# Moving the transposes of the next x, and their evictions, between the second and the third V product

## The chip, the cores and the metric

The kernel runs on one core of a Trainium2 chip. The metric is the device time of one execution in microseconds (us), the median of the runs shown.

## The reference

One layer of gated cross-attention and a quantised feed-forward, for 8 batches of 512 rows and 512 columns (8 x 512 x 512), 16 heads of 32:

```
x = x + tanh(g_xattn) * xattn(layernorm(x), ctx, ctx)
x = x + tanh(g_ffn)   * ffn(layernorm(x))

xattn(query, key, value):
    Q, K, V = query Wq' + bq, key Wk' + bk, value Wv' + bv      # per head
    scores = Q K' / sqrt(32)
    feats  = mean(scores), mean of row maxima, variance of softmax(scores)
    t      = exp(clip(mlp(feats)))                              # one per head
    out    = softmax(Q K' / (2 t)) V
    return out Wo' + bo
ffn(x): quant_act(gelu(quant_act(x) ternary(w1)')) ternary(w2)'
```

## The kernel before

**Turns.** The work on a batch is split into three parts, and a turn `i` does three of them at once: the scores and their statistics for batch `i` (`has_a`), the second scores, values, output product and feed-forward for batch `i - 1` (`has_b`), and the normalisation and the K, V and Q products for batch `i + 1` (`has_p`). Turn -1 has only the products (start-up), turn 0 has no `has_b`, turns 1 to 6 are a hardware loop and have all parts (the text calls them looped turns one to six), turns 7 and 8 have no products. Each engine has its program written out by hand in `body`; nothing is reordered later, and engines meet at semaphores.

**Score tiles.** A score tile is one matmul of 128 x 512 into one of two banks `a_ps` (`score_a`, L1157), its negated row maximum on VectorE (`row_max`, L822), its exponential on ScalarE (`first_exp`, L655) and its statistics on VectorE (`row_stat`, L827). TensorE waits before tile k for the exponential of tile k - 2. Forty of the 64 tiles of a batch run beside the second scores; the rest are "dense": `tiles_a(point)` places 1 or 2 of them ahead of or inside each of the 16 products of a turn, on all three engines in the same order.

**The products.** Behind the second scores come four K products, four output products W0 to W3 (with `has_b`), then the transposes of x and the V products, and four Q products. A K, W, V or Q product is 12 matmuls of 128 x 512 (`split_product`, L1138: high and low halves of fp16 pairs). Between the second and third Q product come the transposes of the quantised residual, `xq`. Each of these writes one of four PSUM banks in turn (`mm_ps` 0 and 1, `b_ps` 0 and 1, in this order banks 0 to 3). `bank_uses` lists the uses of a turn in order and `mm_use` gives for each the bank and how often it was used before: TensorE waits in `take` on `mm_free` of the bank, and the engine that empties it waits on `mm_full`. This list is what sets the bank of a product; the order of the code must agree with it.

**x.** VectorE normalises the next x tile by tile (`norm_x`, L914 and L916), GpSimd makes the low half (`split_x`, L588, `x_lo_done`) and between them adds the output product to the residual (L610). TensorE turns the four tiles (X0 to X3, L1250), 8 transposes of 128 x 128 for each, high and low halves, into one bank, and ScalarE evicts each into `xT` with one instruction of 128 x 1024 (L721). The Q products read `xT` and start when all four are drained. The V products read only the context (`c_hi`, `c_lo`); ScalarE evicts them into `vbuf` (L730).

**VectorE beside the V products.** After the last `norm_x` it takes the statistics of the residual (L883, L1068), then the row maximum of V0's score tile, then the normalised residual (`norm_residual`, L892), the row maximum of V1's tile, the quantisation (`quantise_x`, L897 to L903), and the row maxima of V2's and V3's tiles.

TensorE's order before, in words, per turn: K0 to K3, W0 to W3, X0 to X3, V0 to V3, Q0, Q1, xq, Q2, Q3. ScalarE's: the evictions in the same order, each V eviction behind the exponential of its product's score tile:

```
for t in range(T) if has_p else ():          # X0..X3, L718
    act_waits.wait_ge(mm_full[bank_n], before + 1)
    nc.scalar.activation(xT[...], mm_16[bank_n], ACT.Copy).then_inc(mm_free[bank_n], 1)
for t in range(T):                           # V0..V3, L725
    tiles_a(C + T + t)
    ...
    nc.scalar.activation(vbuf[1 - par][:, t, :], mm_ps[bank_n][:, :], ACT.Copy, ...)
```

Of the kernel before, what the change touches and what calls it, by code (L numbers as in the profile page):

```python
# [31 lines left out]
T = S // P  # L32
# [74 lines left out]
def bank_uses(setup, has_p, has_b, has_a):  # L107

    def some(stage, count, present=True):
        return [(stage, k) for k in range(count)] if present else []  # L110

    uses = some("S", 1, setup == 0) + some("K", C, has_p) + some("W", T, has_b)
    uses += some("X", T, has_p) + some("V", T, has_p)
    uses += some("Q", C, has_p)[:2] + some("xq", T, has_b) + some("Q", C, has_p)[2:]
    uses += some("S", 1, setup == -1)
    uses += some("up0", NB, has_b) + some("up1", NB, has_b) + some("M", 2, has_a)
    for t in range(T):
        if has_b:
            uses += some(f"turn{t}", 2)
            if t > 0:  # L120
                uses += [(f"down{t - 1}", 0)]
            if t + 2 < T:
                uses += some(f"up{t + 2}", NB)
        if has_a and t < 2:
            uses += [("M", 2 + t)]
    uses += some(f"down{T - 1}", 1, has_b)
    return {use: n for n, use in enumerate(uses)}


USES = {-1: bank_uses(-1, True, False, False), 0: bank_uses(0, True, False, True),  # L130
        1: bank_uses(None, True, True, True), 7: bank_uses(None, False, True, True),
        8: bank_uses(None, False, True, False)}
# [11 lines left out]
def mm_use(i, stage, k=0):  # L144

    if isinstance(i, int) and not 1 <= i <= 6:
        n = STARTS[i] + USES[i][stage, k]
        return n % MM, n // MM
    n = STARTS[1] + USES[1][stage, k]
    return n % MM, (i - 1) * (USES_ALL // MM) + n // MM  # L150


def nth(b, per, k):


    return (b + 1) * per + k
# [30 lines left out]
def stages(i):  # L187

    if isinstance(i, int):
        return 0 <= i < B, 1 <= i <= B, i + 1 < B  # L190
    return True, True, True


def flamingo_kernel(nc, x, ctxT, g_xattn, g_ffn, WqT, bq, WkT, bk, WvT, bv, WoT, bo,
                    w1T, b1, w2T, b2, w3T, b3, f1T, f2T, out):
    with ExitStack() as ctx:
# [184 lines left out]
        def dense_tiles(i, point):  # L381

            sets, dense = a_plan(i)
            first = sets + sum(dense[:point])
            return range(first, first + dense[point])
# [243 lines left out]
        def _(act):  # L629
# [21 lines left out]
            def first_exp(b, k):  # L651
                n, t = k // T, k % T
                act_waits.wait_ge(a_max, nth(b, H * T, k + 1))
                act_waits.wait_ge(a_stat, nth(b, H * T, k - 1))
                nc.scalar.activation(etile[:, k % 2, :], a_ps[k % 2][:, :], ACT.Exp,  # L655
                                     bias=nmax[:, slot_of(n), t:t + 1], scale=1.0).then_inc(a_exp, 1)
# [11 lines left out]
            def body(i, par):  # L668
                has_a, has_b, has_p = stages(i)
# [12 lines left out]
                def tiles_a(point):  # L682
                    for k in dense_tiles(i, point) if has_a else ():
                        first_exp(i, k)
# [26 lines left out]
                for t in range(T):  # L711
                    tiles_a(C + t)
                    if has_b:
# [1 line left out]
                        act_waits.wait_ge(mm_full[bank_n], before + 1)  # L715
                        nc.scalar.activation(attn[:, t, :], mm_ps[bank_n][:, :], ACT.Copy,
                                             scale=tg_w[:, 0:1]).then_inc(mm_free[bank_n], 1)
                for t in range(T) if has_p else ():  # L718
                    bank_n, before = mm_use(i, "X", t)
                    act_waits.wait_ge(mm_full[bank_n], before + 1)  # L720
                    nc.scalar.activation(xT[:, :, :, t * P:(t + 1) * P].rearrange("p l c n -> p (l c) n"),  # L721
                                         mm_16[bank_n], ACT.Copy).then_inc(mm_free[bank_n], 1)
                if isinstance(i, int) and i == 0:
                    act_waits.wait_ge(f_tern, 7)
                for t in range(T):  # L725
                    tiles_a(C + T + t)
                    if has_p:
                        bank_n, before = mm_use(i, "V", t)
                        act_waits.wait_ge(mm_full[bank_n], before + 1)
                        nc.scalar.activation(vbuf[1 - par][:, t, :], mm_ps[bank_n][:, :], ACT.Copy,  # L730
                                             scale=1.0 / WSCALE).then_inc(mm_free[bank_n], 1)
# [381 lines left out]
        def _(pe):  # L1113
# [3 lines left out]
            def take(i, stage, k=0):  # L1117

                bank_n, before = mm_use(i, stage, k)
                if not (isinstance(before, int) and before == 0):  # L1120
                    pe_waits.wait_ge(mm_free[bank_n], before)
                return bank_n
# [5 lines left out]
            def split_product(bank_n, left, right, tiles=()):  # L1128


                tiles = list(tiles)
                if tiles:
                    tiles.pop(0)()
                pairs = [(c, l, r) for c in range(C) for l, r in ((0, 0), (0, 1), (1, 0))]
                for c, l, r in pairs:
                    if tiles and (c, l, r) == pairs[len(pairs) // 2]:
                        tiles.pop(0)()
                    ins = mat(mm_ps[bank_n][:, :], left[l](c), right[r](c),  # L1138
                              start=(c, l, r) == pairs[0], stop=(c, l, r) == pairs[-1])
                ins.then_inc(mm_full[bank_n], 1)  # L1140
# [48 lines left out]
            def body(i, par):  # L1189
                has_a, has_b, has_p = stages(i)  # L1190
# [24 lines left out]
                def tiles_a(point):  # L1215
                    return [lambda k=k: score_a(i, par, k) for k in dense_tiles(i, point)] if has_a else []

                def alone(tiles):
                    for tile in tiles:
                        tile()  # L1220
# [16 lines left out]
                for t in range(T):  # L1237
# [3 lines left out]
                                      [lambda c, w=w: w["o"][:, c, :] for w in (w_hi, w_lo)], tiles_a(C + t))  # L1241
                    else:
                        alone(tiles_a(C + t))
                if has_p:
                    for t in range(T):
                        pe_waits.wait_ge(x_lo_done, nth(i + 1, T, t + 1))
                        bank_n = take(i, "X", t)
                        for l in range(2):
                            for c in range(C):
                                ins = nc.tensor.transpose(mm_16[bank_n][:, l * C + c, :],  # L1250
                                                          x_split[t][:, l, c * P:(c + 1) * P], ident16[:, :])
                        ins.then_inc(mm_full[bank_n], 1)
                if first:
                    pe_waits.wait_ge(w_lo_done, 2)
                for t in range(T):
                    rows = slice(t * P, (t + 1) * P)
                    if has_p:
                        split_product(take(i, "V", t), [lambda c, x=x: x(c, rows) for x in c_parts],
                                      [lambda c, w=w: w["v"][:, c, :] for w in (w_hi, w_lo)], tiles_a(C + T + t))
                    else:  # L1260
                        alone(tiles_a(C + T + t))
# [127 lines left out]
```

## Time and profile before

| what | value |
|---|---|
| median of 3 runs | 1525.43 us (1525.19 to 1525.73) |
| span of the profiled execution, first to last instruction | 1523.1 us (its time outside the span is not given apart; the median is 2.3 us above the span) |
| TensorE busy | 1247.1 us (82%), 6620 matmuls |
| VectorE busy | 1187.1 us (78%) |
| ScalarE busy | 958.2 us (63%) |
| GpSimd busy | 429.1 us (28%) |
| mean granted TensorE clock | 0.911 of full speed |

PE is TensorE (PEld its weight loads), DVE VectorE, ACT ScalarE, POOL GpSimd, SP SyncE, whose queue issues the DMAs. Times within the trace count from the first instruction. L1138 is line 1138 of the kernel. `region` stands for several buffers: at L1250 the source `region` is the first half of the x pairs and `x_more` the second half, at L721 `region` is `xT`. Matmuls are pipelined: a row of one matmul shows 0.38 us at full clock while the next starts 0.217 us after it.

### The profile page before, as it was taken

Reading aid. Unit: us, or ns where it says so; the run is one execution under the profiler, and the core shown is the slowest. Engines: PE = TensorE matmul, PEld = TensorE weight load, DVE = VectorE, ACT = ScalarE, POOL = GpSimd, SP = SyncE. Lnnn points to the kernel's source line nnn. Section 1 sums busy time; section 2 is a strip of 40 time slices with the busy share of each in tenths; the row PEclk is TensorE's granted clock in tenths of the full one; section 3 lists DMA queues with packets and bytes.
Section 4 is the critical chain, followed back from the end, with each engine's and each line's share of the span. In section 5 each row is a group of like instructions: output and inputs, shape, how many; then the busy total and the mean of one; then the engine's idle time right before and its main releaser. Section 6 shows DMA issues by size and latency. Waiting matters only on the chain.

```text
span 1523.1 us, 23233 instructions
## 1 busy us (share of the span) xinstructions
PE 1247.1 (82%) x6620; PEld 450.7 (30%) x6620; DVE 1187.1 (78%) x2082; ACT 958.2 (63%) x1559; POOL 429.1 (28%) x389
## 2 busy tenths in 40 slices
PE   3635669988898889988898889988998899778958
PEld 1201321244213332244214331244213431133224
DVE  7399769888788958888788959888688969974236
ACT  3554469755785559755785659755795658744814
POOL 5350342331325212331325213331225211210220
PEclk9855779999999999999999999999999999879979
DMA  8250130012202110012202110112202110001000
GB/s 320 63 159 0 42 86 12 30 41 50 76 2 70 43 72 15 34 37 56 70 2 70 43 72 15 37 34 52 74 2 70 43 56 1 1 0 57 1 0 28
DMA packets 34977, 73.66 MB, mean 48 GB/s; under 512 B 7456, under 2 KB 7456, under 8 KB 34336
## 3 DMA queue, kind: packets, MB, share of 16 engines
q1 hardware_dynamic: 34848, 72.10, 16.1%
q8 instruction: 62, 1.02, 0.3%
q14 instruction: 67, 0.55, 0.1%
HBM read 38.39 MB, written 8.39 MB: 31 GB/s over the span
## 4 chain that ended last, share of the span: by engine, by line
PE 44%; DVE 32%; issue 12%; ACT 6%; POOL 4%; DVEq 1%; DMA 1%; SPq 0%; ACTq 0%; POOLq 0%
DVE stat L827 7%; PE mm_ps L1138 6%; PE b_ps L1312 5%; DVE nmax L822 5%; PE b_ps L1163 5%; PE a_ps L1157 4%; PE b_ps L1138 4%; PE mm_ps L1178 4%; PE mm_ps L1185 3%; ACT etile L655 3%; PE o_ps L1178 3%; PE mm_ps L1291 2%; DVE hmax L952 2%; POOL xres L610 2%; PE b_ps L1291 2%
## 5 line engine op out<-in xcount | busy, mean ns | idle before, releaser
L655 ACT ACTIVATE etile<-a_ps,nmax 128x512 f32<-128x512 f32 x512 | 355.8, 697 | 251.7 <-DVE nmax L822 250.7
L822 DVE TENSOR_REDUCE nmax<-a_ps 128x1 f32<-128x512 f32 x512 | 348.8, 682 | 89.1 <-PE a_ps L1157 81.4
L665 ACT ACTIVATE region<-b_ps,inv2t 128x512 f32<-128x512 f32 x512 | 333.6, 700 | 66.9 <-PE b_ps L1163 63.3
L827 DVE BATCH_NORM_STATS2 stat<-etile 128x6 f32<-128x512 f32 x512 | 350.7, 685 | 15.5 <-ACT etile L655 13.2
L1157 PE MATMUL a_ps<-kst,qst 96*128 96x512 f16 x512 | 213.3, 418 | 105.8 <-ACT etile L655 80.7
L1163 PE MATMUL b_ps<-qst,kst 97*128 97x512 f16 x512 | 198.7, 398 | 24.1 <-ACT region L665 15.1
L583 POOL TENSOR_TENSOR region<-region 128x512 f16<-128x512 f32 x64 | 80.7, 1263 | 307.4 <-ACT region L702 307.2
L1163 PEld LDWEIGHTS b_ps<-qst,kst 97*128 97x128 f16 x512 | 49.3, 97 | 287.5 <-ACT region L665 254.4
L544 POOL TENSOR_TENSOR region<-region 128x512 f32<-128x512 f32 x32 | 40.5, 1267 | 325.2 <-DVE region L855 325.2
L569 POOL TENSOR_TENSOR xres<-xres,bo_row 128x512 f32<-128x512 f32 x32 | 39.7, 1273 | 318.0 <-DMA xres<-in_x_dram 318.0
L1157 PEld LDWEIGHTS a_ps<-kst,qst 96*128 96x128 f16 x512 | 50.6, 99 | 211.1 <-ACT etile L655 168.0
L1312 PE MATMUL b_ps<-f,region 128*128 128x512 fp8e4 x496 | 110.8, 379 | 0.0
L952 DVE TENSOR_REDUCE hmax<-region 128x1 f32<-128x512 f32 x128 | 80.6, 678 | 9.2 <-ACT region L762 8.2
L1178 PE MATMUL mm_ps<-region,vbuf 128*32 128x512 f32 x512 | 73.8, 650 | 0.0
L762 ACT ACTIVATE region<-mm_ps,xmax 128x512 f32<-128x512 f32 x64 | 42.8, 691 | 49.1 <-PE mm_ps L1291 48.8
L1291 PE MATMUL mm_ps<-f,region 128*128 128x512 fp8e4 x256 | 70.0, 421 | 4.3 <-ACT region L745 1.8
L1178 PE MATMUL o_ps<-region,vbuf 128*32 128x512 f32 x512 | 68.2, 605 | 2.3 <-ACT region L665 2.1
L1185 PE MATMUL mm_ps<-region,ones 128*32 128x512 f32 x512 | 70.0, 620 | 0.0
L1185 PE MATMUL z_ps<-region,ones 128*32 128x512 f32 x512 | 68.0, 603 | 0.0
L1291 PE MATMUL b_ps<-f,region 128*128 128x512 fp8e4 x256 | 61.8, 382 | 1.8 <-DVE region L975 1.6
L1312 PEld LDWEIGHTS b_ps<-f,region 128*128 128x128 f16 x496 | 47.5, 98 | 53.1
L981 DVE SCALAR_TENSOR_TENSOR xres<-b_ps,out_scale,xres 128x512 f32<-128x512 f32 x31 | 23.2, 749 | 46.5 <-PE b_ps L1312 46.4
(218 smaller groups left out, 2038.1 us busy)
## 6 DMA issues: line engine op xcount, KB each, us to landing
kst<-region SPq DMA_DIRECT2D x96, 128.0 KB, 2.3
qst<-region SPq DMA_DIRECT2D x96, 128.0 KB, 2.3
region<-in_x_dram SPq DMA_DIRECT2D x8, 1024.0 KB, 5.4
xres<-in_x_dram SPq DMA_DIRECT2D x8, 1024.0 KB, 5.2
out_dram<-xres SPq DMA_DIRECT2D x32, 256.0 KB, 2.0
cin<-in_ctxT_dram SPq DMA_DIRECT2D x30, 256.0 KB, 5.1
kst<-in_f1T_dram SPq DMA_DIRECT2D x2, 1024.0 KB, 11.2
qst<-in_f2T_dram SPq DMA_DIRECT2D x2, 1024.0 KB, 5.4
```

The source lines that it names most:

```text
L655: nc.scalar.activation(etile[:, k % 2, :], a_ps[k % 2][:, :], ACT.Exp, bias=nmax[:, slot_of(n), t:t + 1], scale=1.0).then_inc(a_exp, 1)
L665: nc.scalar.activation(probs[:, s % 2, g, :], b_ps[g % 2][:, :], ACT.Exp, scale=inv2t[:, slot:slot + 1]).then_inc(b_exp, 1)
L822: vec.tensor_reduce(nmax[:, slot_of(k // T), k % T:k % T + 1], a_ps[k % 2][:, :], AX.X, ALU.max, negate=True).then_inc(a_max, 1)
L827: vec.bn_stats(stat[:, slot_of(k // T) * T + k % T, :], etile[:, k % 2, :]).then_inc(a_stat, 1)
L952: ins = vec.tensor_reduce(hmax[:, n:n + 1], hbuf[t % 2][:, n * S:(n + 1) * S], AX.X, ALU.max, apply_absolute_value=True)
L1138: ins = mat(mm_ps[bank_n][:, :], left[l](c), right[r](c), start=(c, l, r) == pairs[0], stop=(c, l, r) == pairs[-1])
L1157: mat(a_ps[k % 2][:, :], qst[par][0:SHIFT, slot, t * P:(t + 1) * P], kst[par][0:SHIFT, slot, :], start=True, stop=True).then_inc(a_full, 1)
L1163: mat(b_ps[g % 2][:, :], kst[par][0:SHIFT + 1, slot, k * P:(k + 1) * P], qst[par][0:SHIFT + 1, slot, :], start=True, stop=True).then_inc(b ...
L1178: mat(oz_ps[G % 2][0][g * DK:(g + 1) * DK, :], vbuf[par][:, k, n * DK:(n + 1) * DK], probs[:, s % 2, g, :], start=k == 0, stop=k == T - 1)
L1185: ins = mat(oz_ps[G % 2][1][g * DK:(g + 1) * DK, :], ones32[:, 0:DK], probs[:, s % 2, g, :], start=k == 0, stop=k == T - 1)
L1291: ins = mat(mm_ps[bank_n][:, :], xqT[:, c, t * P:(t + 1) * P], f1[:, c, n * S:(n + 1) * S], start=c == 0, stop=c == C - 1)
L1312: ins = mat(mm_ps[bank_n][:, :], hT[t % 2][:, k, :], f2[:, k, :], start=k == 0, stop=k == KC - 1)
```

## The change

The four uses "X" move in the bank list from in front of the first V to between the second and the third V. On TensorE the loop over the transposes becomes a function that is called ahead of the third V product (and of its score tile), and on ScalarE the loop over the x evictions becomes a function that is called ahead of the exponential of the third V product's score tile. Nothing else is edited; behind these places the line numbers grow by 4 on ScalarE and TensorE, and by 7 on TensorE behind the loop (L1138 is now L1142, L1250 is L1254, L730 is L734).

```diff
@@ bank_uses
     uses = some("S", 1, setup == 0) + some("K", C, has_p) + some("W", T, has_b)
-    uses += some("X", T, has_p) + some("V", T, has_p)
+    uses += some("V", T, has_p)[:2] + some("X", T, has_p) + some("V", T, has_p)[2:]
     uses += some("Q", C, has_p)[:2] + some("xq", T, has_b) + some("Q", C, has_p)[2:]
@@ scalar
-                for t in range(T) if has_p else ():
+                def turned_x(t):
                     bank_n, before = mm_use(i, "X", t)
                     act_waits.wait_ge(mm_full[bank_n], before + 1)
                     nc.scalar.activation(xT[:, :, :, t * P:(t + 1) * P].rearrange("p l c n -> p (l c) n"),
                                          mm_16[bank_n], ACT.Copy).then_inc(mm_free[bank_n], 1)
+
                 if isinstance(i, int) and i == 0:
                     act_waits.wait_ge(f_tern, 7)
                 for t in range(T):
+                    if has_p and t == 2:
+                        for n in range(T):
+                            turned_x(n)
                     tiles_a(C + T + t)
@@ tensor
-                if has_p:
+                def turned_x():
                     for t in range(T):
                         pe_waits.wait_ge(x_lo_done, nth(i + 1, T, t + 1))
                         bank_n = take(i, "X", t)
...
                         ins.then_inc(mm_full[bank_n], 1)
+
                 if first:
                     pe_waits.wait_ge(w_lo_done, 2)
                 for t in range(T):
                     rows = slice(t * P, (t + 1) * P)
+                    if has_p and t == 2:
+                        turned_x()
                     if has_p:
                         split_product(take(i, "V", t), ...
```

ScalarE in a looped turn, from the last output product's eviction (L716) to the x evictions; `mm_ps0` and `mm_ps1` are banks 0 and 1, `b_ps0` and `b_ps1` banks 2 and 3. This is the difference, where + is the change:

```order
 L716 ACTIVATE region1<-b_ps1,tg_w 128x512 [waits mm_full3]
 L97 REGISTER_ALU
+L97 REGISTER_ALU [waits a_max]
+L655 ACTIVATE etile<-a_ps0,nmax 128x512 [waits a_stat]
+L97 REGISTER_ALU
+L734 ACTIVATE vbuf1<-mm_ps0 128x512 [waits mm_full0]
+L97 REGISTER_ALU
+L97 REGISTER_ALU [waits a_max]
+L655 ACTIVATE etile<-a_ps1,nmax 128x512 [waits a_stat]
+L97 REGISTER_ALU
+L734 ACTIVATE vbuf1<-mm_ps1 128x512 [waits mm_full1]
+L97 REGISTER_ALU
```

Two exponentials and the evictions of V0 and V1 now stand between W3's eviction and X0's.

TensorE in a looped turn, behind W3's last matmul, before the change (L1250 are the transposes, the first two groups of four):

```order
L1138 MATMUL b_ps1<-wo_hi,region4 128x512
L97 REGISTER_ALU
L97 REGISTER_ALU [waits x_lo_done]
L1250 MATMUL mm_ps0<-ident16,region3 128x128 [waits mm_free0]
L1250 MATMUL mm_ps0<-ident16,region3 128x128 x7
L97 REGISTER_ALU
L97 REGISTER_ALU [waits x_lo_done]
L1250 MATMUL mm_ps1<-ident16,region3 128x128 [waits mm_free1]
```

and behind V1's last matmul, with the change (the last two groups of four, and V2's score tile and first product):

```order
L1254 MATMUL mm_ps0<-ident16,x_more 128x128 [waits mm_free0]
L1254 MATMUL mm_ps0<-ident16,x_more 128x128 x7
L97 REGISTER_ALU
L97 REGISTER_ALU [waits x_lo_done]
L1254 MATMUL mm_ps1<-ident16,x_more 128x128 [waits mm_free1]
L1254 MATMUL mm_ps1<-ident16,x_more 128x128 x7
L97 REGISTER_ALU
L97 REGISTER_ALU [waits mm_free2]
L1161 MATMUL a_ps0<-kst0,qst0 128x512 [waits a_exp]
L1142 MATMUL b_ps0<-wv_hi,c_hi 128x512
```

The transposes stood behind W3 and took banks 0 to 3 in this order; now V0 and V1 take banks 0 and 1, X0 and X1 banks 2 and 3, X2 and X3 banks 0 and 1, and V2 and its tile wait for bank 2, which X0 filled.

## Rows read from the trace of the kernel before

**Rows 1.** The page's chain that ended last, share of the span by engine.
```profile
PE 44%; DVE 32%; issue 12%; ACT 6%; POOL 4%; DVEq 1%; DMA 1%; SPq 0%; ACTq 0%; POOLq 0%
```

**Rows 2.** The chain in order of time, looped turn four: start, us, what.
```profile
830.71 0.70 DVE st L883
...
841.57 0.61 DVE nmax L822
...
844.93 1.30 PE mm_ps L1138 x6
```

**Rows 3.** Timeline of TensorE, turn four: start, us, engine, line, op, tiles, count [idle before].
```profile
824.13 1.06 PE L1250 MATMUL mm_ps<-ident,region 128*128 128x128 f16 x16
826.38 0.62 PE L1250 MATMUL b_ps<-ident,x_more 128*128 128x128 f16 x8 [1.20 <-POOL x_more L588]
829.58 1.03 PE L1250 MATMUL b_ps<-ident,x_more 128*128 128x128 f16 x8 [2.58 <-POOL x_more L588]
...
830.83 0.63 PE L1138 MATMUL mm_ps<-wv_hi,c_hi 128*128 128x512 f16 x1
831.26 0.63 PE L1138 MATMUL mm_ps<-wv_lo,c_hi 128*128 128x512 f16 x1
...
843.03 0.39 PE L1157 MATMUL a_ps<-kst,qst 96*128 96x512 f16 x1
843.25 0.60 PE L1138 MATMUL mm_ps<-region,wq_hi 128*128 128x512 f16 x2
```

**Rows 4.** Timeline of ScalarE, turn four, W3's score tile to V2's.
```profile
826.33 0.69 ACT L655 ACTIVATE etile<-a_ps,nmax 128x512 f32<-128x512 f32 x1 [1.93 <-DVE nmax L822]
...
827.49 1.94 ACT L721 ACTIVATE region<-mm_ps 128x1024 f16<-128x1024 f16 x2
...
832.61 0.69 ACT L655 ACTIVATE etile<-a_ps,nmax 128x512 f32<-128x512 f32 x1 [0.94 <-DVE nmax L822]
...
836.44 0.69 ACT L655 ACTIVATE etile<-a_ps,nmax 128x512 f32<-128x512 f32 x1 [1.26 <-DVE nmax L822]
837.39 0.60 ACT L730 ACTIVATE vbuf<-mm_ps 128x512 f32<-128x512 f32 x1 [0.27 <-PE mm_ps L1138]
842.28 0.69 ACT L655 ACTIVATE etile<-a_ps,nmax 128x512 f32<-128x512 f32 x1 [4.29 <-DVE nmax L822]
```

**Rows 5.** Timeline of VectorE, turn four.
```profile
833.60 1.92 DVE L892 TENSOR_SCALAR region<-xres,mv,rstd 128x512 f32<-128x512 f32 x4 [0.50 <-POOL rstd L556]
835.63 0.69 DVE L822 TENSOR_REDUCE nmax<-a_ps 128x1 f32<-128x512 f32 x1
```

**Rows 6.** Timelines of VectorE and TensorE, turns two and five.
```profile
490.70 1.92 DVE L892 TENSOR_SCALAR region<-xres,mv,rstd 128x512 f32<-128x512 f32 x4 [0.50 <-POOL rstd L556]
500.36 0.60 PE L1138 MATMUL mm_ps<-region,wq_hi 128*128 128x512 f16 x2
...
1002.61 0.63 PE L1138 MATMUL mm_ps<-wv_hi,c_hi 128*128 128x512 f16 x1
1005.38 1.92 DVE L892 TENSOR_SCALAR region<-xres,mv,rstd 128x512 f32<-128x512 f32 x4 [0.49 <-POOL rstd L556]
1015.95 0.59 PE L1138 MATMUL mm_ps<-region,wq_hi 128*128 128x512 f16 x2
```

**Rows 7.** Timelines of ScalarE and TensorE, the turn of batch 0.
```profile
171.67 0.69 ACT L655 ACTIVATE etile<-a_ps,nmax 128x512 f32<-128x512 f32 x1 [1.42 <-DVE nmax L822]
...
176.53 1.03 PE L1250 MATMUL b_ps<-ident,x_more 128*128 128x128 f16 x8 [1.07 <-POOL x_more L588]
...
190.53 0.60 PE L1138 MATMUL mm_ps<-region,wq_hi 128*128 128x512 f16 x2
```

**Rows 8.** Timelines of TensorE and ScalarE, start-up: first transposes, key eviction, last V eviction.
```profile
31.67 1.06 PE L1250 MATMUL b_ps<-ident,region 128*128 128x128 f16 x16
37.26 0.86 PE L1250 MATMUL mm_ps<-ident,x_more 128*128 128x128 f16 x8 [4.54 <-ACT region L702]
...
39.43 0.58 PE L1138 MATMUL b_ps<-wv_hi,c_hi 128*128 128x512 f16 x1
...
37.67 0.69 ACT L702 ACTIVATE region<-mm_ps,bqk 128x512 f16<-128x512 f32 x1
...
50.68 0.60 ACT L730 ACTIVATE vbuf<-mm_ps 128x512 f32<-128x512 f32 x1 [1.99 <-PE mm_ps L1138]
```

## The prediction

> **What bounds the kernel now.** First the page's chain: the last-ending work is 44% TensorE and 32% VectorE [rows 1], so the two engines share the bound and a gap on TensorE costs only where no VectorE chain ends behind it. Then the chain in order of time through one looped turn, the fourth of six [rows 2]: from the residual's statistics at 830.71 it runs through VectorE and GpSimd up to the row maximum at 841.57, then changes to TensorE, and stays on TensorE's query products, six matmuls in 1.30 us (0.217 us each, at 2.4 GHz). So the query stage starts when both are ready, and from there its start moves everything behind it.
>
> Then the timelines of that stretch, one engine at a time. TensorE [rows 3]: the x transposes begin at 824.13, and two of the four groups wait for GpSimd's low halves (1.20 and 2.58 us). The V products begin at 830.83 at the lower clock (0.43 us from one to the next), and the query stage's score tile comes at 843.03. ScalarE [rows 4]: the x evictions run from 827.49, the exponentials of the V stage's first, second and third tile at 832.61, 836.44 and 842.28. VectorE [rows 5]: the residual's normalisation starts at 833.60, the second V tile's row maximum at 835.63. The turn's VectorE order holds the score tiles back, and ScalarE evicts V0 only behind the first of these exponentials and V1 only behind the second.
>
> **The change, part by part.** Nothing is added or removed: 32 transposes and 4 evictions change places per batch, and so do the banks. No DMA moves, and SP's queue, GpSimd and VectorE keep their order; their waits for bank releases get other numbers. V0 and V1 keep the first two of the four banks, X0 and X1 take the third and fourth, X2 and X3 the first and second again (which V0 and V1 must have left), V2 and V3 the third and fourth (which X0 and X1 must have left).
>
> *The six looped turns.* What is taken away: TensorE no longer stands 1.20 and 2.58 us for GpSimd in front of V0. V0 starts at 824.2. Its 13 steps (a tile and 12 products) last 2.8 us, V1's tile is let go by the exponential that ends at 827.02 [rows 4], and V1 ends near 829.9. X0 and X1 are ready by then and end near 831. What is added: X2 needs V0's eviction, which comes behind the exponential at 832.61, and X3 needs V1's, behind the one at 836.44. Neither can come earlier, since VectorE's order in front of them is unchanged. TensorE therefore stands some 3 us twice. And the x evictions now queue behind V1's: from the row maximum at 835.63 it is 0.81 us to the exponential, 0.59 to V1's eviction (as from 836.44, one instruction to the next), 0.60 for it [rows 4], 1.03 for X0's (an x eviction by itself, as the two at 827.49 last 1.94 with 0.9 between their starts), and 0.06 to TensorE, as between the exponential's end at 842.97 and the tile at 843.03. So V2, whose bank X0 held, starts 3.1 us behind that row maximum, at 838.7. X3's transposes (8 in 0.52 to 0.86 us from 837.7) are done by then.
>
> Behind that stand V2, V3 and the query tile: 27 steps of 0.217 us, 5.85 us, plus what the clock takes. Before, the 52 steps from the first V product to the first query product, 11.3 us at full clock, took 13.34 us in turn five (1002.61 to 1015.95) [rows 6] and 12.42 in turn four (830.83 to 843.25, the latter 0.22 behind the tile); so restarts cost 1.2 to 2.1 us there, after 2.58 us of standing. Now TensorE has done only 32 transposes in the 8.8 us ahead of V2. I take 1.6 us, with 0 and 5.7 (all 27 steps at 0.43) as far bounds. The first query product then comes 2.03 + 3.1 + 5.85 + 1.6 = 12.58 us behind the start of the residual's normalisation (2.03 is 833.60 to 835.63). For turn four: 846.18 in place of 843.25, 2.93 later. Turns one, three and six repeat turn four within 0.1 us. Turn two: 490.70 + 12.58 = 503.28 against 500.36, 2.92 later. Turn five: 1005.38 + 12.58 = 1017.96 against 1015.95, 2.01 later [rows 6]. Sum over six turns: **+16.6 us**. Nothing hides it: queued on TensorE behind the two waits are V2, V3 and the whole query stage, and for that wait ScalarE's evictions, GpSimd's low halves and the feed-forward. On ScalarE the exponential of V2's tile is queued behind the four x evictions; they end near 841.3, before its row maximum is due (841.57), so it stays where it was.
>
> *The turn of batch 0*, which has no output product and no residual. TensorE stood between the transpose groups for GpSimd, the last from 176.53, and reached the query products at 190.53 [rows 7]. Now V0's tile can start when the exponential of 171.67 has ended, at 172.4; 26 steps, at the lower clock for the first 4.2 us (a loss of 2.1, as in turn five), end near 180.2. V0 and V1 are evicted as they end, for VectorE has no residual work there. The 32 transposes take 2.1 us, V2 starts at 182.4, the first query product comes 5.85 us later, at 188.3: **-2.2 us** (bounds -1 and -3).
>
> *The start-up.* TensorE ended the key products and the first transposes at 32.7 and stood until 37.26, when ScalarE had emptied a key bank; V began at 39.43 and its last eviction at 50.68, behind which ScalarE's start-up chain runs without a gap [rows 8]. Now V0 and V1 fill 31.7 to 36.9. The last key eviction ends at 38.36; V0's, V1's and X0's end at 40.4; V2 starts at 40.5 and V3 ends 5.2 us later, 45.7, plus 0 to 1.7 us at the lower clock. V3's eviction starts near 46.5: **-4.2 us** (bounds -3.2 and -4.8). The chain behind it is ScalarE's sums and VectorE's ternary weights, whose data have landed, so the gain is kept.
>
> Sum: -4.2 - 2.2 + 16.6 = +10.2 us. The trace's span is 1523.1 us, 2.3 under the median of the runs, 1525.4; I keep that difference. **1535.6 us.**
>
> The clock is the one price where a page speaks. In the trace it was at 1.2 GHz after GpSimd's waits, and back at 2.4 by the query products [rows 2, 3]. The Trainium skill, TensorE: Matmul & The Clock Gate, section "A second HAM failure mode: psum-queue depth-cycling", says that short idle times between groups of matmuls which cycle through PSUM banks make the clock swing, and that the work between them pays for it; by that rule the clock's share would grow with this change, which speaks against it. The first rival gives the same mechanism its price from rows.
>
> **The rivals.** (a) *The clock stays down through V2 and V3.* TensorE now has two long waits in a row where it had shorter ones, and enters V2 after 8.8 us with little work. All 27 steps at 0.43 us in place of 0.217 add 5.7 us, not 1.6: 4.1 more in each of six turns, 24.6, and 1560.2 us. Against it: in no turn before did a restart cost more than 2.1 us. Chance 0.08.
>
> (b) *No bank wait: the new place only fills the gap.* If V0 and V1 were out of their banks when TensorE reaches X2 (at 831), TensorE would be at the query tile by 841 and wait for the exponential of 842.28, as now. The looped turns would gain 0 in four, 0.2 in turn two, 0.9 in turn five, and with the two early stages the sum is -7.5: 1517.9 us, faster. It decides at one point: V1's exponential would have to end before 831 instead of at 837.1, so VectorE would have to take its row maximum ahead of the residual's statistics. The order says that it doesn't. What speaks for it is that two waits of 1.20 and 2.58 us do vanish. Chance 0.08.
>
> (c) *The losses are small and the two early stages pay for them.* If V2 and V3 ran at full clock (no 1.6), each turn loses 1.3 (turn five 0.4), 7.0 in all, and the sum is +0.6: 1526.0 us. For it: V0 and V1 now run at full clock. Against it: after less standing than now, the clock was down in every turn. Chance 0.14 (all that ends within 0.2%).
>
> The change does what it says in any case: both engines' orders show it in all eight batches' turns.
>
> **How the numbers follow.** My forecast has 0.70, (a) 0.08, (b) 0.08, (c) 0.14. 0.2%, 3.05 us, is about what a measurement of this kernel can tell from no change. The forecast's own range takes 0.9 to 2.6 us for the clock (6 times -0.7 and +1.0) and the bounds of the early stages: 1530 to 1544. To hold 8 in 10 it must reach half-way to (c) and a little into (a): 1528 to 1547. Faster by over 0.2%: 0.08; within: 0.14; slower: 0.78.
>
> **What would show it.** In a looped turn: V0 starting right behind W3; X2 and X3 waiting for ScalarE's V evictions, some 3 us each; V2's first product 5 us behind the residual's normalisation; four x evictions in a row behind V1's; the query tile waiting for TensorE itself and no longer for the exponential; each looped turn about 2.8 us longer. Batch 0's turn and the start-up shorter by 2 and 4 us. I am wrong if V2 starts before ScalarE has done X0, if the exponentials of the first two V tiles come earlier, or if the query stage starts where it did.

## The result and the profile after

| | before | after |
|---|---|---|
| median of 5 runs each, taken on the same chip | 1525.73 us (1525.19 to 1529.63) | 1536.91 us (1535.29 to 1539.35) |
| ratio of after to before, 95% interval (from all the runs; the two medians by themselves give 1.0073) | | 1.0066 (1.0048 to 1.0084) |
| span of the profiled execution (own time of after's: 1539.35 us) | 1523.1 us | 1537.6 us |
| TensorE busy, VectorE busy | 1247.1, 1187.1 us | 1250.8, 1189.7 us |
| first query product behind the start of the residual's normalisation, mean of six looped turns | 9.81 us | 12.69 us |
| first query product of the start-up | 50.48 us | 46.73 us |
| first output product of turn one | 300.74 us | 296.04 us |

The change makes the kernel slower, by 11.2 us between the medians. The profiled execution of after is the slowest of its five, so its trace shows somewhat more: 14.5 us of span. Runs of the kernel before spread from 1524.5 to 1531.1 us over the chips used here; its trace [rows 1 to 8], with a span of 1523.1 us, is one of the faster ones, while its medians in the comparisons below lie between 1525.4 and 1528.1. So small effects are read from the stages of the traces, and from ratios only with their intervals.

The chain that ended last, by engine, is almost that of before [rows 1]; a share over the whole span doesn't tell what moved. The profile page of after:

```profile
PE 43%; DVE 32%; issue 12%; ACT 6%; POOL 4%; DVEq 1%; DMA 1%; SPq 0%; ACTq 0%; POOLq 0%
```

The list of TensorE's waits tells it (what waited, for whom: us in total, times, longest). Of after:

```profile
PE a_ps L1161 <- ACT etile L655: 84.9, 88, 8.4
PE mm_ps L1254 <- ACT vbuf L734: 35.8, 12, 3.2
```

The first line, of score tiles, was about as long before (80.7 us); the second is new. And in the same list of before stood the wait that the change was to take away:

```profile
PE b_ps L1250 <- POOL x_more L588: 25.3, 14, 2.6
```

The 25.3 us of waiting for GpSimd are gone, and 35.8 us of waiting for ScalarE's evictions of V0 and V1 have come: twelve of them, two in each looped turn.

Looped turn four on TensorE after the change (start, us, engine, line, op, tiles, count, idle before it and who ended it), against [rows 3]:

```profile
830.65 0.38 PE L1142 MATMUL mm_ps<-wv_hi,c_hi 128*128 128x512 f16 x1
...
836.20 1.06 PE L1254 MATMUL b_ps<-ident,region 128*128 128x128 f16 x16
840.16 0.62 PE L1254 MATMUL mm_ps<-ident,x_more 128*128 128x128 f16 x8 [2.91 <-ACT vbuf L734]
843.98 1.03 PE L1254 MATMUL mm_ps<-ident,x_more 128*128 128x128 f16 x8 [3.20 <-ACT vbuf L734]
844.97 0.61 PE L1161 MATMUL a_ps<-kst,qst 96*128 96x512 f16 x1
845.37 0.63 PE L1142 MATMUL b_ps<-wv_hi,c_hi 128*128 128x512 f16 x1
...
848.23 0.38 PE L1142 MATMUL b_ps<-wv_lo,c_hi 128*128 128x512 f16 x1
...
852.12 0.38 PE L1161 MATMUL a_ps<-kst,qst 96*128 96x512 f16 x1
852.34 0.59 PE L1142 MATMUL mm_ps<-region,wq_hi 128*128 128x512 f16 x2
```

V0 starts behind W3 without a wait, V1 and the transposes of X0 and X1 follow without one; then TensorE stands twice, for X2's bank and for X3's. V2's tile comes at 844.97, at the lower clock, and the query tile at 852.12 has nothing in brackets: it waits for TensorE alone.

ScalarE in the same stretch, against [rows 4]:

```profile
838.93 0.69 ACT L655 ACTIVATE etile<-a_ps,nmax 128x512 f32<-128x512 f32 x1 [5.03 <-DVE nmax L826]
839.52 0.59 ACT L734 ACTIVATE vbuf<-mm_ps 128x512 f32<-128x512 f32 x1
842.75 0.69 ACT L655 ACTIVATE etile<-a_ps,nmax 128x512 f32<-128x512 f32 x1 [2.65 <-DVE nmax L826]
843.34 0.59 ACT L734 ACTIVATE vbuf<-mm_ps 128x512 f32<-128x512 f32 x1
843.81 1.94 ACT L721 ACTIVATE region<-b_ps 128x1024 f16<-128x1024 f16 x2
845.62 1.96 ACT L721 ACTIVATE region<-mm_ps 128x1024 f16<-128x1024 f16 x2
848.60 0.69 ACT L655 ACTIVATE etile<-a_ps,nmax 128x512 f32<-128x512 f32 x1 [1.01 <-DVE nmax L826]
```

V0 and V1 were finished on TensorE at 833.4 and 836.4, and ScalarE empties them at 839.52 and 843.34. It had stood idle for 5.03 and 2.65 us ahead of the exponentials in front of them. The two exponentials wait for VectorE, against [rows 5]:

```profile
839.91 1.91 DVE L896 TENSOR_SCALAR region<-xres,mv,rstd 128x512 f32<-128x512 f32 x4 [0.50 <-POOL rstd L556]
841.95 0.69 DVE L826 TENSOR_REDUCE nmax<-a_ps 128x1 f32<-128x512 f32 x1
...
847.80 0.68 DVE L826 TENSOR_REDUCE nmax<-a_ps 128x1 f32<-128x512 f32 x1
849.72 0.69 DVE L826 TENSOR_REDUCE nmax<-a_ps 128x1 f32<-128x512 f32 x1 [0.64 <-PE a_ps L1161]
```

VectorE itself is as far in its order as before: 2.04 us from the residual's normalisation to V1's row maximum, as in [rows 5]. The last row is V3's tile, for which it now waits 0.64 us.

The chain in order of time (start, us, what) strings the three together, against [rows 2]:

```profile
841.95 0.70 DVE nmax L826
...
843.34 0.60 ACT vbuf L734
...
843.98 1.03 PE mm_ps L1254 x8
845.02 0.56 PE a_ps L1161
845.58 3.89 PE b_ps L1142 x12
849.47 0.22 PE a_ps L1161
849.69 2.59 PE b_ps L1142 x12
852.28 0.22 PE a_ps L1161
852.50 1.30 PE mm_ps L1142 x6
```

Before, the chain changed from VectorE to TensorE at V2's row maximum, with the query products next [rows 2]. Now it leaves VectorE one tile earlier, at V1's, goes through ScalarE's eviction of V1, and has X3, V2 and V3 between that and the query products. V2's twelve products last 3.89 us and V3's 2.59: of the first, 1.30 us is clock.

### The profile page after: what moved, and what is told of

Read it like the earlier page. It is cut to its first block, busy times and chain, and to the rows that moved or that the text cites. A ratio compares the mean times of both kernels' runs of the same rounds, so it can differ in the third digit from the quotient of the medians.

```text
span 1537.6 us, 23233 instructions
## 1 busy us (share of the span) xinstructions
PE 1250.8 (81%) x6620; PEld 450.9 (29%) x6620; DVE 1189.7 (77%) x2082; ACT 957.2 (62%) x1559; POOL 428.1 (28%) x389
## 4 chain that ended last, share of the span: by engine, by line
PE 43%; DVE 32%; issue 12%; ACT 6%; POOL 4%; DVEq 1%; DMA 1%; SPq 0%; ACTq 0%; POOLq 0%
DVE stat L831 7%; DVE nmax L826 5%; PE b_ps L1319 5%; PE b_ps L1167 5%; PE b_ps L1142 5%; PE mm_ps L1142 5%; PE a_ps L1161 4%; PE mm_ps L1182 4%; PE mm_ps L1189 3%; ACT etile L655 3%; PE o_ps L1182 2%; PE mm_ps L1298 2%; POOL xres L610 2%; DVE hmax L956 2%; PE b_ps L1298 2%
## 5 line engine op out<-in xcount | busy, mean ns | idle before, releaser
L1167 PE MATMUL b_ps<-qst,kst 97*128 97x512 f16 x512 | 198.0, 396 | 24.2 <-ACT region L665 15.2
L985 DVE SCALAR_TENSOR_TENSOR xres<-b_ps,out_scale,xres 128x512 f32<-128x512 f32 x31 | 23.2, 749 | 46.5 <-PE b_ps L1319 46.4
```

The costliest lines, as they stand in the source:

```text
L1167: mat(b_ps[g % 2][:, :], kst[par][0:SHIFT + 1, slot, k * P:(k + 1) * P], qst[par][0:SHIFT + 1, slot, :], start=True, stop=True).then_inc(b ...
```

## The experiments

Each result below is a median, beside the median of the kernel before on the same chip. Line numbers differ by a few from kernel to kernel. The time from the start of the residual's normalisation to the first query product, in a looped turn, is called the **query delay**: 9.65 us before (10.57 in turn five), 12.2 to 13.1 after.

### The change in the two early stages alone, and in the looped turns alone

`has_b` is true in the looped turns and false in the start-up and batch 0's turn. In the first kernel the transposes move only there:

```diff
-                    if has_p and t == 2:
+                    if has_p and t == (2 if not has_b else 0):
                         turned_x()
```

(with the same condition in ScalarE's loop and in `bank_uses`), and in the second the condition is turned round.

> Only the turns without a value part (start-up and batch 0) have the transposes of x and their evictions behind the second V product; the six looped turns are as before the change. Theory (two gains, one loss): the start-up and batch 0's turn end 4.7 us earlier, as in the trace of the change, and the looped turns take what they took: about 1520.7 us, 4.7 under the kernel before. Rival (the gain of the early turns is taken up by a later wait, or the trace's 4.7 us is clock chance): within 1.5 us of the kernel before.

Measured: 1522.58 us beside 1528.14, ratio 0.9968 (0.9955 to 0.9981), 5.6 us faster, near the 4.7 expected. In its trace the first output product of turn one comes at 292.60, 8.1 us earlier than before, but the span is only 2.3 us shorter (1520.8 us): the query delay is 9.66 us in three looped turns and 10.6 to 10.8 in the other three, 2.2 us more in sum, and the stages behind it take 3.6 us more. In those three turns it is 13.4 to 13.6 us from the first V product to the first query product, as in turn five before (13.34 [rows 6]); why is open.

> Only the six looped turns have the change; start-up and batch 0's turn are as before it. Theory: each looped turn loses 2.5 to 3.5 us between the residual's normalisation and the first query product, 17.3 in all, so 15 to 18 us over the kernel before, about 1542 us, and 4 to 5 us over the change. Rival (the loss depends on what the early turns do, by the phase of the clock): no more than 11 us over the kernel before, as the whole change.

Measured: 1542.45 us beside 1528.14, ratio 1.0093 (1.0077 to 1.0108), 14.3 us slower, a little less than the 15 to 18 expected. The query delays sum to 75.77 us, against 76.12 after the whole change and 58.84 before.

So the change is two changes of opposite sign, and the sum of the two, +8.7 us between the medians, is near the 11.2 of the whole (by the ratios, +0.61% against +0.66%). The gain of the early stages varies from trace to trace: in the eight traces here that have the new place there, the first output product of turn one lies between 292.60 and 296.04.

### Is it the wait for the two banks, or ScalarE's order?

The profile names the waits of X2 and X3. Here these two get banks of their own, in `o_ps` and `z_ps`, which are idle beside these products, and TensorE no longer waits for banks 0 and 1 there; ScalarE reads the new banks in the same order, and nothing else moves:

```diff
-                        bank_n = take(i, "X", t)
+                        bank_n = take(i, "X", t) if t < 2 else mm_use(i, "X", t)[0]
+                        turned = mm_16[bank_n] if t < 2 else oz_16[t - 2]
```

> The change, with the transposes of the third and fourth x tile written to two PSUM banks that are idle there (those of the last heads' outputs and denominators), so that TensorE doesn't wait for the evictions of V0 and V1; ScalarE's order is that of the change. Theory T2 (ScalarE's order is the price: X0's eviction, and so V2's bank, comes behind the exponential of V1's score tile): V2 still starts 3 us behind the second tile's row maximum, the time stays within 2 us of the change, about 1537 us; the two waits of 2.9 and 3.2 us become one wait in front of V2. Theory T1 (TensorE's waits for the banks of V0 and V1 are the price): V2 starts right behind the transposes, the looped turns lose nothing, and the time is 1518 to 1522 us.

Measured: 1537.15 us beside 1528.14, ratio 1.0055 (1.0041 to 1.0069). TensorE in turn four of this kernel:

```profile
833.67 1.06 PE L1257 MATMUL b_ps<-ident,region 128*128 128x128 f16 x16
834.56 0.61 PE L1257 MATMUL o_ps<-ident,x_more 128*128 128x128 f16 x8
835.01 0.61 PE L1257 MATMUL z_ps<-ident,x_more 128*128 128x128 f16 x8
842.45 0.60 PE L1163 MATMUL a_ps<-kst,qst 96*128 96x512 f16 x1 [6.83 <-ACT region L722]
```

Both waits are gone and one of 6.83 us stands in their place, in front of V2, for X0's eviction. The query delays sum to 77.76 us, no less than with the change. The two waits that were new in the list were not what the time hung on. (Turn six alone lost more than with the change, 13.81 us of delay against 12.15, at a mean granted clock of 0.65 from V2's tile to the query products, against 0.81.)

The next kernel adds to this one ScalarE's order: in the looped turns it evicts X0 to X3 behind V0 and ahead of V1's exponential. (GpSimd adds the bias to V0 and V1 when their banks are released; since the x evictions now stand ahead of V1's and count on the same semaphores, GpSimd waits for one release more. This is in the edit too.)

```diff
-                    if has_p and t == 2:
+                    if has_p and t == (1 if has_b else 2):
```

> As the run with two more banks, and in the looped turns ScalarE evicts the four x tiles behind V0's eviction and ahead of the exponential of V1's score tile. Theory T2: V2's bank is free some 1.2 us behind the start of the residual's normalisation in place of 5, V2 and V3 end before the exponential of V2's score tile, and the query tile waits for it, 9.4 us behind that start, as in the kernel before: 1519 to 1522 us, under both kernels. Rival T3 (the lower clock behind the gap is most of the loss): V2 and V3 still run at 1.2 GHz and the query products start 11 us or more behind that start, over 1527 us.

Measured: 1520.74 us beside 1528.14, ratio 0.9945 (0.9931 to 0.996). The query delay is 9.65 or 9.66 us in all six turns. TensorE in turn four:

```profile
831.46 0.39 PE L1163 MATMUL a_ps<-kst,qst 96*128 96x512 f16 x1 [3.01 <-ACT region L722]
...
839.65 0.39 PE L1163 MATMUL a_ps<-kst,qst 96*128 96x512 f16 x1 [0.73 <-ACT etile L656]
```

V2's tile waits 3.01 us in place of 6.83 and the query tile waits for the exponential of V2's tile, as before the change. So the place of X0's eviction in ScalarE's queue is what the looped turns pay for. This is also what rival (b) described: with the price gone, the query delays sum to 57.94 us against 58.84 before, all of the difference from turn five, since VectorE's chain ends there at the same point, and the early stages' gain is left.

### The other end of the same chain: VectorE's order

ScalarE stands for VectorE, which takes V0's and V1's row maxima behind the residual's statistics and behind its normalisation. With the change both tiles are ready long before. Here the banks and ScalarE's order are those of the change, and VectorE takes V0's maximum ahead of the last statistics and V1's ahead of the normalisation:

```diff
                 if has_b:
+                    tiles_a(C + T)
                     c.link(residual_stat(i, T - 1))
...
                     ins.then_inc(mv2_done, 1)
+                    tiles_a(C + T + 1)
...
-                    tiles_a(C + T + t)
+                    if not has_b or t >= 2:
+                        tiles_a(C + T + t)
```

> The change, and in the turns with a residual VectorE takes the row maximum of V0's score tile ahead of the residual's last statistics and that of V1's tile ahead of the residual's normalisation. Four banks as in the change. Theory T2 (V2's bank comes behind V1's exponential, and that behind VectorE's row maximum): V1's exponential comes 3 to 4 us earlier, V2's score tile 1.2 us behind the start of the residual's normalisation in place of 5.1, the query products 8.3 to 9.5 us behind it: the 17 us of the looped turns are gone, and up to 7 more: 1513 to 1521 us where the kernel before takes 1525.5. Rival (TensorE's clock is down behind any gap there and V2 and V3 need 11 us of it): over 1527 us.

Measured: 1512.8 us beside 1527.76, ratio 0.9901 (0.9886 to 0.9916): 15 us faster than before, the lowest median here (two later kernels are not told apart from it). The query delay is 8.38 us in four turns, 8.37 and 8.77 in the others, and V2's tile comes 1.24 us behind the normalisation, as expected. Turn four on TensorE:

```profile
828.18 0.62 PE L1257 MATMUL mm_ps<-ident,x_more 128*128 128x128 f16 x8 [2.46 <-ACT vbuf L734]
829.17 0.39 PE L1164 MATMUL a_ps<-kst,qst 96*128 96x512 f16 x1 [0.37 <-ACT region L721]
...
836.09 0.39 PE L1164 MATMUL a_ps<-kst,qst 96*128 96x512 f16 x1 [1.13 <-ACT etile L655]
836.31 0.60 PE L1145 MATMUL mm_ps<-region,wq_hi 128*128 128x512 f16 x2
```

X2 no longer waits, X3 waits 2.46 us, and the query tile waits for V2's exponential again, 1.27 us earlier behind the normalisation than before (9.65 less 8.38): the row maximum and the statistics of V1's tile no longer stand between the two. They cost nothing where they are now. From the first output product to the normalisation it is 20.5 to 20.8 us in each looped turn, as before; VectorE stood idle there for GpSimd (1.89 us ahead of the last residual statistics in the trace of after, 0.70 here).

Is that VectorE's order by itself, or does it need the change? The same edit on the kernel before:

> The kernel before with the VectorE order alone, the control. Theory: TensorE's 52 steps behind the fourth x tile end no earlier than now, so the looped turns gain at most 0.2 us each (turn five 0): within 2 us of the kernel before. Rival (the VectorE order alone is worth as much as in the other two): 5 to 8 us under it.

Measured: 1533.61 us beside 1527.76, ratio 1.0041 (1.0027 to 1.0055), slower. The expectation missed. The query delay is 8.36 us as hoped, but the way from the first output product to the normalisation has grown to 23.1 to 24.2 us: with the transposes ahead of V0, V0's and V1's tiles come late, and VectorE, which takes them in its own order, stands for them with the normalisation queued behind. Turn four on VectorE, the row maxima of V0's and V1's tiles:

```profile
835.72 0.69 DVE L822 TENSOR_REDUCE nmax<-a_ps 128x1 f32<-128x512 f32 x1 [1.64 <-PE a_ps L1160]
...
840.22 0.69 DVE L822 TENSOR_REDUCE nmax<-a_ps 128x1 f32<-128x512 f32 x1 [2.09 <-PE a_ps L1160]
```

I had counted only the gain behind the normalisation.

### Both orders together, and where TensorE stands

If ScalarE's order saves something and VectorE's does, both should save at least as much as either:

> The run with two more banks and ScalarE's order, with the same VectorE order. Theory: ScalarE's x evictions now start behind V0's eviction some 3 us earlier, V2 starts before the residual's normalisation, and the query tile waits for the exponential of V2's score tile alone, 8.3 us behind that start: about 7 us under the run without the VectorE order, 1512 to 1516 us on a chip where the kernel before takes 1525.5. Rival (VectorE is the bound of the query stage, and gives the 1.2 us per turn back there): within 2 us of the run without it.

Measured: 1523.37 us beside 1527.76, ratio 0.997 (0.9959 to 0.9981). This missed too: 1512 to 1516 us where the kernel before takes 1525.5 would be a ratio of 0.991 to 0.994. The query delays sum to 50.79 us, as good as the 50.66 with VectorE's order alone; the loss lies behind them. From the first query product to the next turn's first output product the six turns take 864.1 us, against 853.8 there. Turn four on TensorE:

```profile
838.89 0.61 PE L1166 MATMUL a_ps<-kst,qst 96*128 96x512 f16 x1 [3.78 <-ACT etile L656]
839.29 1.06 PE L1147 MATMUL mm_ps<-region,wq_hi 128*128 128x512 f16 x2
```

and the busy times of the engines from there (stretch and its length; TensorE, weight loads, VectorE, ScalarE, GpSimd; then the granted clock of TensorE):

```profile
839.00:843.00 4.00, 4.00 (x12) 1.44 (x12) 2.50 (x5) 2.18 (x4) 0.00 (x0) 0.58 0.00 0
```

V2 and V3 end early, TensorE stands 3.78 us directly in front of the query stage, and over the four us from there the mean granted clock is 0.58, for the most part the lower of the two levels (1.2 GHz of 2.4). From the query tile to the second score tile behind it TensorE takes 4.66 to 4.72 us in the six turns, and 3.03 or 3.04 in those of the kernel with VectorE's order alone. That is 10.0 us in sum, of the 10.3 lost. The next kernel takes ScalarE's order alone back out of this one: VectorE's new order and the two more banks stay, the x evictions come behind V1's again, and so V2 starts late again. If the loss comes from where TensorE stands, it should vanish:

> The run with ScalarE's and VectorE's order, with ScalarE's x evictions put back behind V1's eviction, as in the change: TensorE keeps the two more banks, and V2 waits again for X0's eviction. It asks why that run missed. Theory (place of the gap): an earlier V2 only moves TensorE's standing from in front of V2 to in front of the query tile, where it grows to 3.8 us, and the clock is down in the first query product, with no slack behind; with V2 held back TensorE stands in front of V2, is warm again by the query stage, and the time is that of the change with VectorE's order, 7 to 11 us under the missed run, 1511 to 1516 us. Rival (the two more banks or the changed waits themselves cost): within 3 us of the missed run, about 1523 us.

Measured: 1513.22 us beside 1525.37, ratio 0.9907 (0.9888 to 0.9926). Turn four, TensorE:

```profile
827.89 0.39 PE L1166 MATMUL a_ps<-kst,qst 96*128 96x512 f16 x1 [3.01 <-ACT region L722]
...
834.81 0.39 PE L1166 MATMUL a_ps<-kst,qst 96*128 96x512 f16 x1 [1.13 <-ACT etile L656]
```

and its stretch from the query stage on, in the same columns:

```profile
834.00:838.00 4.00, 3.19 (x15) 1.48 (x16) 4.00 (x7) 3.40 (x6) 0.00 (x0) 1.00 0.00 0
```

TensorE stands for 3.01 us ahead of V2 and 1.13 ahead of the query tile, 4.14 in all against 0.27 and 3.78, 4.05, in the kernel with both orders. The sum is nearly the same and its place differs, and here the query stage runs at the full clock. (The two kernels differ in ScalarE's order too, by which the place is set, and in GpSimd's two waits, so the place by itself is not isolated; the query delays, 51.43 and 50.79 us in sum, don't explain the ten microseconds, and the time lost at the lower clock does.)

In turn four the clock stayed up behind the 3.01 us. In turns one, three and five it fell, within V2, as here in turn three:

```profile
657.83 0.39 PE L1166 MATMUL a_ps<-kst,qst 96*128 96x512 f16 x1 [3.01 <-ACT region L722]
...
659.28 0.63 PE L1147 MATMUL b_ps<-wv_hi,c_lo 128*128 128x512 f16 x1
...
665.14 0.38 PE L1166 MATMUL a_ps<-kst,qst 96*128 96x512 f16 x1
```

From V2's tile to the query tile it is 7.31 us at a mean granted clock of 0.77, and at full clock V2 and V3 need 5.6 (26 steps of 0.217): 1.7 us lost, as much as in the kernel with both orders. But the wait of 1.13 us ahead of the query tile takes up most of it, and the query delay is 8.76 us in place of 8.38. So a fall of the clock in V2 and V3 is mostly covered by slack; in the query stage nothing covers it.

At last one more row maximum is taken ahead, V2's behind the normalisation and ahead of the quantisation:

```diff
-                    if not has_b or t >= 2:
+                    if not has_b or t > 2:
                         tiles_a(C + T + t)
                     if has_b and t == 0:
                         norm_residual(i - 1, c, has_p)
+                        tiles_a(C + T + 2)
```

> The change with VectorE's order, and the row maximum of V2's score tile too taken ahead of the quantisation. Theory (VectorE bounds the query stage by now): the query tile comes 1.1 us earlier, but its second tile waits for the exponential of V3's, whose maximum stays behind the quantisation, and is 0.2 to 0.3 us earlier at most: within 2 us of the run without it, 1511 to 1514 us. Rival (TensorE bounds it and each turn gains the 1.1 us): 6 us under it, about 1507 us.

Measured: 1513.16 us beside 1525.37, ratio 0.9909 (0.989 to 0.9927), not told apart from 0.9901 without this step, as expected. In turns three and five the query tile waits for nothing and the delay is 7.08 us, but the second tile of the query stage then stands for V3's exponential (0.89 us in turn three), and comes 9.42 us behind the normalisation against 9.68. Over the six turns the query delays sum to 47.55 us, 3.1 less than without this step, and the stages behind them take 856.5 us, 2.7 more. The start of the query stage has stopped being what sets the turn's length.

## Why the prediction was right

The forecast was 1535.6 us in a range of 1528 to 1547; 1536.9 was measured. The mechanism came as forecast. That the number is so close is in part luck: the trace, the slowest of five executions, moved by 14.5 us where the sum said 10.2, and the terms that were off are named below. Step by step:

**What bounds the stage.** Right. The chain that I read in [rows 2] ran through VectorE's order up to the query products, and after the change it runs through the same row maxima, ScalarE and TensorE, as the sum had it.

**The looped turns, +16.6 us.** Right in mechanism and size: +17.3 in the trace of after (76.12 less 58.84). The parts, in turn four: V2's tile 3.1 us behind V1's row maximum, measured 3.02 (841.95 to 844.97); 27 steps of 5.85 us plus 1.6 us of clock, measured 7.37 us from 844.97 to 852.34, so 1.5 for the clock; V2's exponential stays where it was, measured 8.69 us behind the normalisation against 8.68 in [rows 4, 5]. The mean delay was to be 12.58 us and is 12.69. One precaution made the size right: the two waits that the change adds were not simply summed. They are 6.1 us in turn four, but it lost 2.8, because V0 and V1 are done beforehand and TensorE had stood for GpSimd before. The kernel with two more banks confirms this: without these waits the loss is the same. The kernel with ScalarE's order confirms which queue it is.

**The clock.** The estimate of 1.6 us between 0 and 5.7 came from the restarts in turns four and five of before, and held (0.2 of the 1.2 us in turn four was no restart: V3's last product starts at 842.60, and the query tile, at 843.03, waited for the exponential that ended at 842.97): over the six turns the delays of 12.15 to 13.13 us leave 1.2 to 2.2 us for it, at 2.03, 3.02 and 5.86 for the rest. Rival (a), all 27 steps at the lower clock, did not come: V2's tile and its first seven products ran so or nearly so, and the clock was back by 848.23. The Trainium skill, TensorE: Matmul & The Clock Gate, section "A second HAM failure mode: psum-queue depth-cycling", says that short idle times between groups of matmuls make the clock swing and cost throughput. The trace agrees that it swings: the mean granted clock from V2's tile to the query products is 0.71 to 0.81 in the six turns. But the loss didn't grow with the standing: in turn four it is 1.5 us after two waits of 2.91 and 3.20 us, 1.5 after one of 6.83 with the two more banks, and 1.7 after one of 3.78 in the kernel with both orders. What differed in price was its place.

**The early stages, -4.2 and -2.2 us.** Here the size was off in this trace: together -4.7 at the first output product of turn one, in place of -6.4. The start-up gave -3.75 (V3's eviction at 46.93, against 50.68 before and the 46.5 estimated). X2, X3 and then part of V2 ran at the lower clock:

```profile
39.00 1.78 PE L1254 MATMUL b_ps<-ident,x_more 128*128 128x128 f16 x16
```

Sixteen transposes in 1.78 us, where 1.06 is usual [rows 8]; my bound of 0 to 1.7 us held. With the change in the early stages alone the same sixteen took 1.09 us, and V3's eviction came at 45.69. Batch 0's turn gave -2.2, as forecast, if counted from the statistics of its x on. Between the two some 1.5 us went back, against "the gain is kept". The second six products of K0 in this turn, in the chain of before,

```profile
146.38 1.51 PE mm_ps L1138 x6
```

and of after:

```profile
142.64 2.50 PE mm_ps L1142 x6
```

The products come 3.74 us earlier and TensorE is at the lower clock for nearly all six of them, not for little more than one, which costs 1.0 us. VectorE won 0.4 of it back, where it had waited for a score tile before, and lost 1.0 in one instruction on the ternary weights (L1012, 3.32 us from 158.05, where the same one, L1008, took 2.35 before). The statistics of x, behind them, so come only 2.21 us earlier (161.30 against 163.51). What brought the clock down and what made that instruction longer stays open; no run isolates either. Over the eight traces with the new place in these stages the gain lies between 4.7 and 8.1 us, so -6.4 was in the middle of what they do.

**The stages behind.** I had counted nothing there; they take 852.1 us in place of 849.9 over the six turns, 2.2 more. Single turns differ by 2.3 us less to 1.5 more, so this is not told apart from scatter, and no run isolates it.

**The rivals.** (b) named the point that decides, whether V1's exponential comes early; the order that I read from VectorE said no, and it came 2.84 us behind the start of the normalisation, exactly as before (842.75 less 839.91). Moved ahead on purpose it turned the change into a gain. Of the 0.2 and 0.9 us that (b) foresaw for turns two and five, ScalarE's order gave 0 and 0.9. (c) needed the clock to cost nothing; it cost 1.2 to 2.2 us per turn. The sum of parts measured in the trace, -4.7, +17.3 and +2.2, is +14.8 us, of which the span shows 14.5; the medians show 11.2 and the forecast said 10.2. So in this trace the early stages were mis-sized by 1.7 us, the looped turns by 0.7, and 2.2 were not counted.

## What to carry to other kernels

When work that uses a ring of banks is moved, the question is not only whether the engine that moves has its input, but who empties the bank it will meet next, and what stands ahead of that in the emptying engine's own queue. Here a wait of 3.8 us for GpSimd was exchanged for one on evictions that were ready to run but queued behind exponentials that another engine's order held back; the same move paid as soon as the two row maxima at the root of that chain were moved with it, and that second move alone, without the first, cost time. A wait that is new in the list is not by that the cause: giving the two groups other banks left the time as it was.

## What was not expected of the hardware

Nearly the same standing time of TensorE cost more or less by where it lay. With 3.78 us of it directly ahead of the query stage the mean granted clock in the next four us was 0.58 in turn four and the kernel took 1523.4 us; with 3.01 us ahead of V2 and at most 1.13 ahead of the query stage the clock in that stage was 1.00 and the kernel took 1513.2 us. A faster feeder that let TensorE finish early and stand in front of the critical stage lost some 10 us that way, nearly all of it at the lower clock. And the early stages differ from trace to trace with the same program text in them: in the four kernels that have it (the change, the change in the early stages alone, and the two with VectorE's order and four banks) the first output product of turn one came from 292.60 to 296.04 us, and the start-up's first query product at 45.49 to 46.73, the sixteen transposes of X2 and X3 taking 1.09 us where it came early and 1.78 where it came late.
